# Local attention with the order of rotary and normalisation exchanged: products from PSUM, the norms multiplied in on GpSimd

## The reference, cut to what matters

```python
def l2norm(t):
    return t / jnp.maximum(jnp.linalg.norm(t, axis=-1, keepdims=True), 1e-12)
...
q = l2norm(q) * qs
k = l2norm(k) * ksc
freqs, scale = rotary_tables(n)
cos, sin = (jnp.cos(freqs), jnp.sin(freqs))
q = q * cos * scale + rotate_half(q) * sin * scale
inv = 1.0 / scale
k = k * cos * inv + rotate_half(k) * sin * inv
out = local_attention(q, k, v)
```

## Time and profile before

| | |
|---|---|
| runs of the kernel | 6148.74, 6134.6 and 6152.13 us, median 6148.74 |
| span of the profiled execution, first to last instruction | 6149.6 us |
| mean granted TensorE clock of the span | 0.955 of full speed |
| PE, DVE, ACT, POOL busy | 88%, 73%, 64%, 48% of the span |
| local stacks | the L940 instructions start at 1293.3 to 3529.4 us (`f`) and 3825.8 to 6062.7 us (`g`), 384 in each |

### The profile page before, as it was taken

The page is one execution under the profiler, slowest core; times in us unless marked ns, Lnnn a source line. Parts: engine busy times, 40 slices in busy tenths (PEclk is TensorE's granted clock), DMA queues, the critical chain, the costliest instruction groups (busy, mean ns, idle before and its releaser), DMA issues. The chain is left out here.

```text
span 6149.6 us, 136606 instructions
## 1 busy us (share of the span) xinstructions
PE 5406.4 (88%) x39332; PEld 3486.8 (57%) x39332; DVE 4478.0 (73%) x8145; ACT 3905.8 (64%) x12160; POOL 2939.1 (48%) x2878
## 2 busy tenths in 40 slices
PE   5999999969899898998989956998989989899897
PEld 1222232246666666666666644666666666666665
DVE  7666666468688686886868844886868868688685
ACT  1555555647577575775757721775757757577575
POOL 2000000056566565665656612665656656566564
PEclk6999999989999999999999976999999999999999
DMA  0000000021222212122121211222222221222213
GB/s 12 1 1 1 1 1 1 1 80 46 73 51 58 60 46 72 48 60 60 46 72 46 62 47 56 50 58 61 50 67 51 58 61 48 70 51 58 61 46 87
DMA packets 332449, 288.38 MB, mean 47 GB/s; under 512 B 149246, under 2 KB 290852, under 8 KB 329892
## 3 DMA queue, kind: packets, MB, share of 16 engines
q1 hardware_dynamic: 331172, 282.34, 17.8%
q10 hardware_dynamic: 768, 0.02, 0.0%
HBM read 100.83 MB, written 30.41 MB: 21 GB/s over the span
## 5 line engine op out<-in xcount | busy, mean ns | idle before, releaser
L426 DVE TENSOR_REDUCE a_maxima<-a_bank 128x1 f32<-128x512 f32 x1024 | 677.7, 689 | 346.6 <-PE a_bank L541 342.7
L349 ACT ACTIVATE a_pex<-a_bank 128x512 f32<-128x512 f32 x1024 | 556.3, 596 | 415.3 <-PE a_bank L548 415.3
L1000 ACT ACTIVATE g_ex<-g_bank,g_nmx 128x96 f32<-128x96 f32 x1536 | 501.4, 338 | 345.4 <-DVE g_nmx L1082 345.4
L1000 ACT ACTIVATE f_ex<-f_bank,f_nmx 128x96 f32<-128x96 f32 x1536 | 501.4, 338 | 343.0 <-DVE f_nmx L1082 343.0
L935 POOL TENSOR_TENSOR f_rn<-f_sg,f_minus_half 128x8 f32<-128x8 f32 x384 | 640.2, 1667 | 32.0
L935 POOL TENSOR_TENSOR g_rn<-g_sg,g_minus_half 128x8 f32<-128x8 f32 x384 | 639.7, 1666 | 32.0
L940 POOL TENSOR_TENSOR f_qr<-f_t 128x512 f32<-128x512 f32 x384 | 547.6, 1426 | 14.8 <-DVE f_t L1101 13.1
L559 PE MATMUL a_bank<-a_pex,a_v_head 128*32 128x512 f32 x2048 | 544.3, 610 | 1.7 <-DVE a_osum L443 1.4
L940 POOL TENSOR_TENSOR g_qr<-g_t 128x512 f32<-128x512 f32 x384 | 537.3, 1399 | 14.8 <-DVE g_t L1101 13.1
L1177 PE MATMUL g_bank<-g_wqkv,g_xT 128*128 128x512 f32 x768 | 426.9, 639 | 87.4 <-DVE g_qh L1092 62.1
L1177 PE MATMUL f_bank<-f_wqkv,f_xT 128*128 128x512 f32 x768 | 427.1, 639 | 87.1 <-DVE f_qh L1092 61.8
(11 more groups left out here) (235 smaller groups left out, 13321.6 us busy)
## 6 DMA issues: line engine op xcount, KB each, us to landing
f_vw<-f_vt SPq DMA_DIRECT2D x96, 384.0 KB, 4.2
g_vw<-g_vt SPq DMA_DIRECT2D x96, 384.0 KB, 4.3
f_vw<-f_vt SPq DMA_DIRECT2D x96, 256.0 KB, 3.6
g_vw<-g_vt SPq DMA_DIRECT2D x96, 256.0 KB, 3.6
f_vw<-f_vt SPq DMA_DIRECT2D x96, 128.0 KB, 2.3
g_vw<-g_vt SPq DMA_DIRECT2D x96, 128.0 KB, 2.3
f_wqkv<-in_f_Wqkv_dram SPq DMA_DIRECT2D x7, 1536.0 KB, 7.7
g_wqkv<-in_f_Wqkv_dram SPq DMA_DIRECT2D x7, 1536.0 KB, 9.4
```

The costliest lines, as they stand in the source:

```text
L349: last = act.activation(pex[:, b, e, :], ps_s[2 * b + e][:], ACT.Exp)
L426: dve.tensor_reduce(maxima[:, m // 4, m % 4:m % 4 + 1], ps_max[m % 2][:], AX.X, ALU.max).then_inc(dv_max, 1)
L1000: last = act.activation(ex[:, b, u, :], ps_s[:, KEYS * u:KEYS * u + KEYS], ACT.Exp, bias=nmx[:, b, u:u + 1], accum_out=sm[:, b, u:u + 1])
```

## The change

The normalised intermediate `qh` and its DVE instruction are left out. DVE forms the rotary products from the PSUM bank itself; POOL adds them into `qu` and then multiplies `qu` by `rn`, broadcast over the 64 columns of a head, into `qr`. The bank is freed by the second product and the square (`dv_t2`, `act_sq`), where it was freed by `dv_qh`. POOL waits for its own add (`pl_sum`) and its own powers (`pl_rn`) ahead of the multiply.

```diff
 # GpSimd
                         pool.tensor_scalar(sg[:, b, :], ss[:, b, :], 1e-24, None, ALU.max).then_inc(pl_sg, 1)
                         pool.wait_ge(pl_sg, upto(pl_sg, L, n))
-                        pool.wait_ge(dv_qh, upto(dv_qh, L, n - 2))
+                        pool.wait_ge(pl_qr, upto(pl_qr, L, n - 2))
                         pool.tensor_tensor(rn[:, b, :], sg[:, b, :], minus_half[:], ALU.pow).then_inc(pl_rn, 1)
...
                         pool.wait_ge(dv_t2, upto(dv_t2, L, n - 1))
                         pool.wait_ge(pe_qkT, upto(pe_qkT, L, n - 3))
-                        pool.tensor_tensor(qr[:, 1 - b, :], t1[:, 1 - b, :], t2[:, 1 - b, :], ALU.add).then_inc(pl_qr, 1)
+                        pool.tensor_tensor(qu[:, 1 - b, :], t1[:, 1 - b, :], t2[:, 1 - b, :], ALU.add).then_inc(pl_sum, 1)
+                        pool.wait_ge(pl_sum, upto(pl_sum, L, n - 1))
+                        pool.wait_ge(pl_rn, upto(pl_rn, L, n - 1))
+                        pool.tensor_tensor(qr[:, 1 - b, :].rearrange("p (h d) -> p h d", h=8),
+                                           qu[:, 1 - b, :].rearrange("p (h d) -> p h d", h=8),
+                                           rn[:, 1 - b, :].unsqueeze(2).broadcast_to([P, 8, DH]), ALU.mult).then_inc(pl_qr, 1)
 # VectorE
-                        dve.wait_ge(pl_rn, upto(pl_rn, L, n - 1))
-                        dve.tensor_tensor(heads(qh[:, 1 - b, :]), heads(ps_qk[1 - b][:]),
-                                          rn[:, 1 - b, :].unsqueeze(2).broadcast_to([P, 8, DH]), ALU.mult).then_inc(dv_qh, 1)
...
-                        dve.wait_ge(dv_qh, upto(dv_qh, L, n - 1))
-                        dve.wait_ge(pl_qr, upto(pl_qr, L, n - 3))
-                        dve.tensor_tensor(heads(t1[:, 1 - b, :]), heads(qh[:, 1 - b, :]),
+                        dve.wait_ge(pe_qkv, upto(pe_qkv, L, n - 1))
+                        dve.wait_ge(pl_sum, upto(pl_sum, L, n - 3))
+                        dve.tensor_tensor(heads(t1[:, 1 - b, :]), heads(ps_qk[1 - b][:]),
                                           rope[:, 2 * KIND[cj], row(tj), :].broadcast_to([P, 8, DH]), ALU.mult)
-                        dve.tensor_tensor(split(t2[:, 1 - b, :]), split(qh[:, 1 - b, :])[:, :, ::-1, :],
+                        dve.tensor_tensor(split(t2[:, 1 - b, :]), split(ps_qk[1 - b][:])[:, :, ::-1, :],
                                           rope[:, 2 * KIND[cj] + 1, row(tj), :].broadcast_to([P, 8, DH]).rearrange(
                                               "p h (a b) -> p h a b", a=2), ALU.mult).then_inc(dv_t2, 1)
 # TensorE, before the QKV matmul (and likewise at m == 1 of the MLP)
-                        pe.wait_ge(dv_qh, upto(dv_qh, L, n - 2))
+                        pe.wait_ge(dv_t2, upto(dv_t2, L, n - 2))
+                        pe.wait_ge(act_sq, upto(act_sq, L, n - 2))
```

More of the change, by code:

```diff
@@ L692, in local_stack @@
         rn = sb("rn", [P, 2, 8])
-        qh = sb("qh", [P, 2, 512])
+        qu = sb("qu", [P, 2, 512])
         t1 = sb("t1", [P, 2, 512])
@@ L734, in local_stack @@
         pe_v, act_v = sem("pe_v", 2 * NT, 3), sem("act_v", 2 * NT, 1)
-        pe_qkv, act_sq, dv_ssq = sem("pe_qkv", STEPS), sem("act_sq", STEPS), sem("dv_ssq", STEPS, 2)
-        pl_sg, pl_rn, dv_qh, dv_t2, pl_qr = (sem("pl_sg", STEPS), sem("pl_rn", STEPS, 2), sem("dv_qh", STEPS, 2),
-                                             sem("dv_t2", STEPS), sem("pl_qr", STEPS, 2))
+        pe_qkv, act_sq, dv_ssq = sem("pe_qkv", STEPS), sem("act_sq", STEPS, 2), sem("dv_ssq", STEPS, 2)
+        pl_sg, pl_rn, pl_sum, dv_t2, pl_qr = (sem("pl_sg", STEPS), sem("pl_rn", STEPS, 2), sem("pl_sum", STEPS, 2),
+                                             sem("dv_t2", STEPS, 2), sem("pl_qr", STEPS, 2))
         pe_qkT, act_kprev, act_qk = sem("pe_qkT", STEPS, 2), sem("act_kprev", STEPS // 2), sem("act_qk", STEPS, 1)
@@ L907, in _ @@
         def _(pool):
-            for s in (pl_rn, pl_qr):
+            for s in (pl_rn, pl_sum, pl_qr):
                 pool.sem_inc(s, ahead[s.num])
@@ L972, in _ @@
         def _(act):
-            for s in (act_v, act_exp, act_qk, act_pT, act_aT, act_fT):
+            for s in (act_sq, act_v, act_exp, act_qk, act_pT, act_aT, act_fT):
                 act.sem_inc(s, ahead[s.num])
@@ L1061, in _ @@
         def _(dve):
-            for s in (dv_ssq, dv_qh, dv_y, dv_pn, dv_kzero, dv_xn, dv_fy, dv_ag):
+            for s in (dv_ssq, dv_t2, dv_y, dv_pn, dv_kzero, dv_xn, dv_fy, dv_ag):
                 dve.sem_inc(s, ahead[s.num])
@@ L1089, in tile @@
                     if real(t, c, 1):
-                        dve.wait_ge(pl_rn, upto(pl_rn, L, n - 1))
-                        dve.tensor_tensor(heads(qh[:, 1 - b, :]), heads(ps_qk[1 - b][:]),
-                                          rn[:, 1 - b, :].unsqueeze(2).broadcast_to([P, 8, DH]), ALU.mult).then_inc(dv_qh, 1)
-                    if real(t, c, 1):
                         tj, cj = t + (c - 1) // 4, (c - 1) % 4
-                        dve.wait_ge(dv_qh, upto(dv_qh, L, n - 1))
-                        dve.wait_ge(pl_qr, upto(pl_qr, L, n - 3))
-                        dve.tensor_tensor(heads(t1[:, 1 - b, :]), heads(qh[:, 1 - b, :]),
+                        dve.wait_ge(pe_qkv, upto(pe_qkv, L, n - 1))
+                        dve.wait_ge(pl_sum, upto(pl_sum, L, n - 3))
+                        dve.tensor_tensor(heads(t1[:, 1 - b, :]), heads(ps_qk[1 - b][:]),
                                           rope[:, 2 * KIND[cj], row(tj), :].broadcast_to([P, 8, DH]), ALU.mult)
-                        dve.tensor_tensor(split(t2[:, 1 - b, :]), split(qh[:, 1 - b, :])[:, :, ::-1, :],
+                        dve.tensor_tensor(split(t2[:, 1 - b, :]), split(ps_qk[1 - b][:])[:, :, ::-1, :],
                                           rope[:, 2 * KIND[cj] + 1, row(tj), :].broadcast_to([P, 8, DH]).rearrange(
@@ L1244, in group @@
                 if known and m == 1:
-                    pe.wait_ge(dv_qh, upto(dv_qh, L, STEPS - 1))
+                    pe.wait_ge(dv_t2, upto(dv_t2, L, STEPS - 1))
+                    pe.wait_ge(act_sq, upto(act_sq, L, STEPS - 1))
                     pe.wait_ge(act_qk, upto(act_qk, L, STEPS - 1))
```

## The result

The changed kernel takes 6447.07 us (median of 4 runs, 6440.5 to 6462.45) against 6148.95 for the kernel before: 1.049 times as long, 95% interval 1.0472 to 1.0509. The profiled execution spans 6448.1 us, 298.5 more than before.

A forecast was written before the change was run, and what follows sets the result against it. The prediction took chains passing between engines as the limit. POOL's longer chain and the later bank release add 2.0 us a tile, 33.6 a layer, 403 over 12 layers to 6149.6: 6552 us, 6.6% slower, range 6385 to 6670.

The forecast's parts named there:

- No engine is full; chains set a tile: Mid-layer row tiles of 20.17 and 20.21 us: PE's intervals sum to 18.8, so chains passing between engines set the time.
- L1092's removal brings nothing on PE: DVE loses 0.68 us a step, which alone gains nothing on PE, since DVE has 2.3 to 3.3 us a tile spare.
- The bank release, S + 2.66: PE's next QKV matmul waits for DVE's second product, 2.66 us after the score matmuls end (S), 0.68 later than before.
- The multiply, 1.26: POOL's new broadcast multiply takes 1.26 us, 1.34 with its wait, bounds 0.5 and 1.63, delaying the result PE waits for.
- POOL's idle time is no cover: POOL's idle 1.7 us a step lies after its add, while PE waits for the result, so the multiply still delays it.
- The collision goes away: DVE's weights normalisation no longer overlaps POOL's add, which returns 0.6 us a tile; the new products cannot be hit.
- the walk: Step-by-step timing of one tile from PE's, POOL's and the bank's waits: 19.61 us before the change, where 20.2 was seen.
- The sum: Tile of 22.21 us, 2.0 more; 15 tiles plus 3.4 us of ends make 33.6 a layer, 403 over 12 layers.
- Only the bank release counts: Rival with POOL's multiply nearer 0.5 us: tile of 21.45 us, +247 us, 6396 us; chance 0.13.
- main case: POOL's longer chain and the later bank release together give 6552 us, own range 6510 to 6640; chance 0.66.
- Faster: Rival: POOL's idle 1.7 us hides the multiply's 1.34 and relieved DVE sets the pace, -108 us, 6041 us; chance 0.05.

The follow-up runs named there:

- experiment 3: Changed kernel with PE's transposes of `qr` at the end of its step and ScalarE's copy of `ps_o` ahead of the transposes' copy: 6268.37 us, ratio 1.0198.
- experiment 4: Changed kernel with DVE's products and POOL's add and multiply moved one step ahead (half n in step n): 5827.71 us, ratio 0.9476.
- experiment 2: Kernel before plus a POOL multiply by broadcast ones after the add, bank release untouched: 6454.17 us, ratio 1.0503.
- experiment 6: Kernel before with PE's transposes of `qr` at the step's end, plus a wait so POOL's add starts after DVE's weights normalisation: 5907.82 us, ratio 0.9598.
- Experiment 5: Kernel before with PE's transposes of `qr` moved to the end of the step: 6040.17 us, ratio 0.9819.
- experiment 7: Changed kernel with DVE's products one step ahead, so the bank is free early, POOL's add and multiply left in place: 6464.02 us, ratio 1.051.
- experiment 1: Changed kernel without POOL's multiply, queries and keys left unnormalised: 6247.64 us, ratio 1.0164.
- experiment 8: Changed kernel with a further POOL multiply by ones, all 512 columns, between the add and the multiply by the norms: 7089.08 us, ratio 1.1521.
- experiment 9: Changed kernel with a further POOL multiply by ones, 256 columns, result unused, between add and multiply: 6661.96 us, ratio 1.0837.

## Why the prediction was right, point by point

- **No engine is full; chains set a tile.** Right. Experiments 3 and 4 gained 179 and 619 us from the changed kernel without taking work away.
- **L1092's removal brings nothing on PE.** Not run by itself; that DVE's busy time fell by a fifth and the kernel slowed down fits it.
- **The bank release, S + 2.66.** Right as a mechanism (steps of 5.03 us in three runs), the size 0.1 to 0.2 too large: measured S + 2.57 and S + 2.43, since PE started 0.05 after the product where 0.13 was taken, and in the second step the row maxima started earlier. Two such steps in a tile took 5.03 for 5.21 each, 0.36 of the excess of 0.65 us a tile.
- **The multiply, 1.26.** The mis-sized term: 1.045. The nearest row was POOL's multiply with a broadcast over rows; this one broadcasts one number over 64 columns. The lower bound of 0.5 covered it. It makes 0.22 us a tile of the excess, since the longer loop counts POOL once.
- **POOL's idle time is no cover.** Right, and shown by experiment 2.
- **The collision goes away.** Right: L1081 at 0.569 us in the mean, and the new products at 0.681 even in experiment 4, where POOL's add runs beside them. On this the trace agrees with the Trainium skill, "SBUF — State Buffer", "Who interferes with whom": one SBUF input, no contention. In the changed kernel itself the products run beside the power, and that shows nothing, since the old products with two SBUF inputs were not delayed by it either (0.69 us at 2507.30). That the collision made up the 0.6 us which the walk lacked was argued only; experiment 6 shows that a collision of this kind costs 0.73 us a tile when the transposes are late. Experiment 5 shows that PE's wait for `qr` was part of the loss of before as well.
- **The sum.** 22.21 us a tile were forecast, 21.56 came. 15 tiles times 0.65, over 12 layers, are 117 us of excess, about the 105 by which the forecast was high. The 3.4 us for a layer's ends were about right as a size (the 23.7 us of the layer looked at, less 15 tiles at 1.36, leave 3.3), but lie near its start; the interval from the last L932 of a layer to the next layer's first did not grow, so the late result charged at a layer's end is not seen.
- **The rivals.** "Only the bank release counts" gave 6396 us (its own terms add to 249, not 247), and 6447 is nearer to it than to the main case: the number alone would not have told the two apart. Its mechanism is refuted all the same: experiment 7, without the late release, is as slow and has settled tiles of 21.23 us, experiment 1, without the multiply, takes 6248, and experiment 2, with the multiply alone, 6454. "Faster" needed PE not to wait for the result; it waits.

## What to carry to other kernels

Idle time on an engine covers a moved operation only if nobody is waiting for the result that it delays; here POOL's 1.7 us a step lay after that result, while PE waited for it. Look for which wait a new data dependence removes: this change freed the rotation from the norms, and it turned from a loss of 5% into a gain of 5% only when the freed instructions were moved a step ahead. Compare such a gain with what the old kernel reaches when its own order is mended: experiment 6 is already 4.0% faster than before, so what the change added to that is 1.3%. Costs of two chains that meet at one engine were not added here: the longer one was paid.

## What the runs showed of the hardware that was not expected

- GpSimd's multiply of 128x512 with one number broadcast over each 64 columns took 1.045 us, against 1.27 for the add of two full tiles and 1.26 for the multiply whose broadcast runs over rows; of 256 columns 0.615.
- In experiments 7 and 8, where PE waits 1.5 us and more in one piece, stretches at the 1.2 GHz level appeared in mid-layer (granted clock 0.50 in 2 us windows, a mean of 0.93 over some tiles), in which a QKV matmul of 1.02 us took 1.66. The length of the wait alone does not decide: the same 1.58 us in other tiles of experiment 7, and 1.53 us in the settled tiles of experiment 9, were followed by a clock of 1.00.
- GpSimd's `max` of 128x8 took 0.24 us alone and 0.55 in steps of experiment 4 in which it began while DVE's product of two SBUF inputs was running (POOL at 2615.77, DVE from 2615.49 to 2616.22). From 2600 to 3200 us of that run all 39 that began so took 0.55, the other 63 took 0.23 or 0.24, so the exclusion reaches 8-element reads as well.
- GpSimd's power of 128x8, 1.67 us long, did not delay DVE: products of two SBUF inputs that began and ended while it ran took 0.68 or 0.69 us (in the kernel before, 132 of them in 400 us). So the exclusion for a whole instruction, as the prediction puts it, is not seen with this one.
